# Self-attention of a transformer block: one copy of keys and queries, sums by accumulating DMAs, blocks of eight and eight score matmuls

## Chip, core and metric

The kernel runs on one core of a Trainium2 chip. The metric is the device time of one execution in microseconds (us).

## The reference, cut to what matters

```python
def block_forward(x, codebook_embeds, codebook_mask, ...):
    xn = layer_norm(x, ln0_w, ln0_b)
    q, k, v = jnp.split(xn @ qkv_w.T, 3, axis=-1)
    q, k, v = (_heads(q), _heads(k), _heads(v))          # 16 heads of 32 features
    attn = jnp.einsum('bhnd,bhmd->bhnm', q, k) * SCALE
    attn = jax.nn.softmax(attn, axis=-1)
    x = x + _merge(jnp.einsum('bhnm,bhmd->bhnd', attn, v)) @ sa_proj_w.T
    ...
```

`x` is 2 batches of 2048 tokens with 512 features, in float32. A cross-attention with 154 keys and an MLP follow. The change touches the softmax attention of the tokens among themselves alone, `self_phase`.

## The kernel before

The kernel is a row of phases with a barrier between them: `token_phase` (norm and products for queries, keys and values), `self_phase`, `context_phase`, `token_phase`, the cross `attention_phase`, `token_phase`, `mlp_phase`. Every float32 operand of a product is carried as a high and a low part.

`self_phase` works through 32 stages. A stage is 512 queries (`TOK`) of one batch for four heads (a group of 128 features, each head on its own 32 features), against all 2048 keys; four stages share the keys of a group (`stages_per_group`). A stage i has these parts, and the engines run them as an order written out by hand, each engine in its own function with waits on semaphores:

- **First pass** (`first_pass`, L1466, matmul L1472): scores with the queries in rows, 64 matmuls of 96x128 weights against 512 keys. VectorE (`maxima`, L1585) reduces each to a maximum per query (L1591). The results lie in `first`, a ring of three PSUM banks (`ring`, `in_ring`), and `slot_free` says which reduce has to be over before a slot is written again. `turn_max` (L1475) transposes the maxima in a slot of the same ring, `split_max` (L1598) splits them in two parts, and two DMAs (`load_max`, L1351, on SyncE's queue) lay them as rows 96 and 97 beside the queries.
- **Second pass** (`second_pass`, L1480, matmul L1489): the scores again with the keys in rows, less the maxima by the two extra rows, 64 matmuls of 98x128 weights against 512 queries. ScalarE (L1562) takes the exponential of each into `expo`, a ring of eight key tiles of four heads. `second` too is a ring of three PSUM banks.
- **Values** (`weigh`, L1492, matmul L1500): one key tile of exponentials against the values, four matmuls of 32 columns side by side for the four heads, accumulated in `weighted`. Such a float32 matmul shows as two records in the profile, so a group is x8 there.
- **Sums** (GpSimd's `add_pairs`, L1443; `add_up`, L1504, matmul L1510): GpSimd adds the exponentials of two key tiles (eight "pair" adds of 128x2048 elements, L1453) and merges some pairs once more (two "merge" adds, L1457). TensorE adds each of the six results over the keys, as four matmuls with ones side by side, into `total`.
- **Finish**: VectorE inverts `total` in four pieces (`invert`, L1606, L1610) and multiplies (`divide`, L1612, L1616), ScalarE having copied the weighted values (`take_weighted`, L1565); SyncE stores (`store_out`).

TensorE's order (`period`, L1523) sets the rest: a stage is 16 blocks (`blocks`); a block alternates four first-pass matmuls with four second-pass matmuls (`per_block`), and `batch` (L1514) closes it with the value group of one key tile and, after the blocks that `sums_after` names, a sum:

```python
                def period(i, with_last, with_next, with_after):
                    for j in range(blocks):
                        for at in range(per_block):
                            of, n = first_of[j][at]
                            if with_next if of == 1 else with_after:
                                first_pass(i + of, n)
...
                            second_pass(i, j * per_block + at)
                        batch(i, j, with_last, True)
```

The first pass runs ahead: in the blocks of stage i stand the first-pass matmuls of stage i + 1 from its seventeenth on, and in the last four blocks the first sixteen of stage i + 2; the turn of the maxima lies in block 12. VectorE's four inverse pieces stand in blocks 3 to 6 and the division in block 7, each after the block's second reduce. SyncE's queue loads keys and queries twice, once for each pass (`k_move`, `q_hold` for the first, `k_hold`, `q_move` for the second), each as three copies of 32 rows (high, high, low or high, low, high), and issues each load when the waits in its order have passed.

Of the kernel before, what the change touches and what calls it, by code (L numbers as in the profile page):

```python
# [6 lines left out]
P = 128  # L7
ALU = mybir.AluOpType
ACT = mybir.ActivationFunctionType
F32 = mybir.dt.float32  # L10
# [6 lines left out]
TOK = 512  # L17
# [1169 lines left out]
def self_phase(nc, name, q_t, k_t, v, out, batches):  # L1187
# [16 lines left out]
    blocks = n_k  # L1204
    per_block = heads
# [5 lines left out]
    pair_slots = 4  # L1211
# [6 lines left out]
    sum_ready = [pool_ops.index(("merge", p) if ("merge", p) in pool_ops else ("pair", p)) + 1 for p in summed]  # L1218
    n_sums = len(summed)
    sums_after = {1: [(-1, 4)], 2: [(-1, 5)], 8: [(0, 0)], 9: [(0, 1)], 11: [(0, 2)], 15: [(0, 3)]}  # L1220
    slot_sum = {0: [0, 3], 1: [1], 2: [4], 3: [2, 5]}
# [31 lines left out]
    with ExitStack() as stack:  # L1253
        m = Memory(nc, stack, name)
        k_move = m.sbuf("k_move", [P, heads, keys], F32R)
        k_hold = m.sbuf("k_hold", [P, heads, keys], F32R)
        q_hold = m.sbuf("q_hold", [P, heads, TOK], F32R)
        q_move = m.sbuf("q_move", [P, 2, heads, TOK], F32R)
# [19 lines left out]
        k_move_loaded = [m.sem(f"k_move_loaded{a}") for a in range(heads)]  # L1278
        k_hold_loaded = [m.sem(f"k_hold_loaded{j}") for j in range(4)]
        v_loaded = [m.sem(f"v_loaded{j}") for j in range(4)]  # L1280
        q_hold_loaded = [m.sem(f"q_hold_loaded{a}") for a in range(heads)]
        q_move_loaded = m.sem("q_move_loaded")
# [8 lines left out]
        pool_done = m.sem("pool_done")  # L1291
# [16 lines left out]
        with nc.Block() as block:  # L1308

            @block.sync  # L1310
            def _(sp):
# [8 lines left out]
                def load_k_move(g, a):  # L1320
                    b, group = group_of(g)
                    stacked(k_move[:, a:a + 1], k_t, (0, 0, 1), bass.ds(group * P + a * HEAD_DIM, HEAD_DIM),
                            bass.ds(b * keys, keys), k_move_loaded[a])

                def load_k_hold(g, j):
                    b, group = group_of(g)
                    k0, n = j * k_set * P, k_set * P
                    stacked(k_hold[:, :, k0:k0 + n], k_t, (0, 0, 1), bass.ds(group * P, P), bass.ds(b * keys + k0, n),
                            k_hold_loaded[j])
# [720 lines left out]
```

## Time and profile before

| | before |
|---|---|
| median of 3 runs (lowest to highest) | 3913.47 us (3911.08 to 3914.4) |
| the profiled execution, its own time | 3913.35 us |
| its span, first to last instruction | 3911.6 us |
| TensorE busy in the span | 3591.7 us (92%) |
| VectorE, ScalarE, GpSimd busy | 2221.3, 1601.9, 1731.8 us |
| reduces L1591 | 2048, 1265.2 us busy |
| exponentials L1562 | 2048, 1074.2 us busy |
| score matmuls L1472 and L1489 | 2048 and 2048 |
| value matmuls L1500, records | 4096, 545.5 us busy |
| sum matmuls L1510, records | 1536, 201.6 us busy |
| GpSimd's adds L1453 and L1457 | 256 and 64, 1170.2 and 293.4 us busy |

A busy time counts an engine once however many of its instructions overlap; matmuls are pipelined, so the time from one start to the next says more than their duration. An "idle before" with an arrow names what ended the wait. The self-attention spans about 316 to 2168 us.

### The profile page before, as it was taken

The numbers are of one execution on the slowest core, as the hardware profiler recorded it, in microseconds if no ns is written. First come the engines' busy times: TensorE is split into PE (matmuls) and PEld (weight loads), VectorE is DVE, ScalarE is ACT, GpSimd is POOL, SyncE is SP. The second block draws the span as 40 slices with busy tenths as digits, with TensorE's granted clock in tenths as the row PEclk, the third lists the DMA queues.
The fourth block names the chain that finished last, engine by engine and source line by source line (L and its number), as shares of the span: only waits on it lengthen the run. The fifth ranks groups of instructions, "written<-read, shape, count | busy, mean of one in ns | idle before, by whom it ended". The sixth has DMA issues, their size and how long they took to land. (4 is left out here: it accounts for less than half of the span.)

```text
span 3911.6 us, 57974 instructions
## 1 busy us (share of the span) xinstructions
PE 3591.7 (92%) x17160; PEld 2143.7 (55%) x17160; DVE 2221.3 (57%) x3649; ACT 1601.9 (41%) x2855; POOL 1731.8 (44%) x415
## 2 busy tenths in 40 slices
PE   7998999999999999999999499599996859999999
PEld 6884444444444444444443377334332748888887
DVE  4446777777777777778773344345553743222222
ACT  3221666666666666666566233033333331111111
POOL 0001878887888788878888121132233300000000
PEclk9996999999999999999999699555555979999999
DMA  4546132232313132232410434865743662111110
GB/s 168 181 156 155 36 88 50 69 74 59 80 44 87 41 81 63 65 74 53 92 32 9 157 133 168 181 131 123 149 91 107 240 223 88 43 44 43 43 43 22
DMA packets 197952, 370.25 MB, mean 95 GB/s; under 512 B 28706, under 2 KB 53048, under 8 KB 188652
## 3 DMA queue, kind: packets, MB, share of 16 engines
q1 hardware_dynamic: 197868, 369.15, 34.0%
q8 instruction: 50, 0.82, 0.1%
q14 instruction: 34, 0.28, 0.0%
HBM read 248.68 MB, written 119.34 MB: 94 GB/s over the span
## 5 line engine op out<-in xcount | busy, mean ns | idle before, releaser
L1591 DVE TENSOR_REDUCE self_part_max<-self_first 128x1 f32<-128x512 f32 x2048 | 1265.2, 680 | 378.4 <-PE self_first L1472 375.5
L1562 ACT ACTIVATE self_expo<-self_second 128x512 f32<-128x512 f32 x2048 | 1074.2, 602 | 754.6 <-PE self_second L1489 754.6
L1453 POOL TENSOR_TENSOR self_pair_sum<-self_expo 128x2048 f32<-128x2048 f32 x256 | 1170.2, 4576 | 365.6 <-ACT self_expo L1562 365.6
L1472 PE MATMUL self_first<-self_k_move,self_q_hold 96*128 96x512 f32 x2048 | 895.2, 444 | 31.3 <-DVE self_part_max L1591 18.8
L1489 PE MATMUL self_second<-self_q_move,self_k_hold 98*128 (+1 forms) x2048 | 812.4, 400 | 4.3 <-ACT self_expo L1562 4.2
L1472 PEld LDWEIGHTS self_first<-self_k_move,self_q_hold 96*128 96x128 f32 x2048 | 393.9, 193 | 587.7 <-DVE self_part_max L1591 308.9
L1500 PE MATMUL self_weighted<-self_expo,self_v_sb 128*32 128x512 f32 x4096 | 545.5, 604 | 10.0 <-issue 10.0
L1489 PEld LDWEIGHTS self_second<-self_q_move,self_k_hold 98*128 98x128 f32 x2048 | 388.7, 191 | 84.7 <-ACT self_expo L1562 24.8
L1943 DVE CAST mlp_h_high<-mlp_h 128x512 fp32r<-128x512 f32 x128 | 54.7, 427 | 504.6 <-PE mlp_out_sum L61 504.6
L1918 ACT ACTIVATE mlp_h<-mlp_hidden_sum,mlp_b_col 128x512 f32<-128x512 f32 x128 | 88.0, 688 | 601.0 <-PE mlp_hidden_sum L61 601.0
L937 POOL TENSOR_TENSOR cross_pair_sum<-cross_expo 77x2048 f32<-77x2048 f32 x32 | 144.7, 4521 | 358.8 <-ACT cross_expo L1072 358.8
L1457 POOL TENSOR_TENSOR self_pair_sum<-self_pair_sum 128x2048 f32<-128x2048 f32 x64 | 293.4, 4585 | 5.0
L1072 ACT ACTIVATE cross_expo<-cross_second 77x512 f32<-77x512 f32 x256 | 144.4, 590 | 301.7 <-PE cross_second L992 301.4
L59 PE MATMUL mlp_hidden_sum<-mlp_xt_high,mlp_w_high 128*128 128x512 f32 x512 | 201.2, 393 | 24.1 <-DMA mlp_xt_low<-xn_t 24.1
L968 PEld LDWEIGHTS cross_first<-cross_k_move,cross_q_hold 98*128 98x128 f32 x512 | 137.8, 318 | 148.7 <-issue 83.8
L968 PE MATMUL cross_first<-cross_k_move,cross_q_hold 98*128 98x154 f32 x512 | 152.2, 422 | 62.2 <-DMA cross_k_move<-mask_rows 39.7
L1510 PE MATMUL self_total<-self_pair_sum,self_ones 128*32 128x512 f32 x1536 | 201.6, 595 | 5.1 <-POOL self_pair_sum L1453 5.1
L1124 DVE TENSOR_REDUCE cross_row_max<-cross_first 128x2 f32<-128x308 f32 x256 | 115.6, 472 | 159.3 <-PE cross_first L968 157.7
L59 PE MATMUL mlp_out_sum<-mlp_w_high,mlp_h_high 128*128 128x512 f32 x512 | 202.6, 396 | 0.0
L60 PE MATMUL mlp_out_sum<-mlp_w_low,mlp_h_high 128*128 128x512 f32 x512 | 202.5, 396 | 0.0
L61 PE MATMUL mlp_hidden_sum<-mlp_xt_high,mlp_w_low 128*128 128x512 f32 x512 | 202.5, 395 | 0.0
L61 PE MATMUL mlp_out_sum<-mlp_w_high,mlp_h_low 128*128 128x512 f32 x512 | 202.4, 395 | 0.0
(163 smaller groups left out, 4187.7 us busy)
## 6 DMA issues: line engine op xcount, KB each, us to landing
self_q_hold<-q_t SPq DMA_DIRECT2D x384, 64.0 KB, 2.1
self_k_move<-k_t SPq DMA_DIRECT2D x96, 256.0 KB
self_q_move<-q_t SPq DMA_DIRECT2D x96, 256.0 KB, 4.5
self_k_hold<-k_t SPq DMA_DIRECT2D x96, 256.0 KB, 4.7
cross_q_hold<-cq_t SPq DMA_DIRECT2D x24, 1024.0 KB, 12.0
cross_q_move<-cq_t SPq DMA_DIRECT2D x24, 1024.0 KB, 14.5
qkv_x<-in_x SPq DMA_DIRECT2D x8, 1024.0 KB, 5.7
v<-qkv_v_sb SPq DMA_DIRECT2D x32, 256.0 KB, 2.0
```

The source lines that it names most:

```text
L59: nc.tensor.matmul(out, left_high, right_high, start=first, stop=False)
L60: nc.tensor.matmul(out, left_high, right_low, start=False, stop=False)
L61: return nc.tensor.matmul(out, left_low, right_high, start=False, stop=last)
L968: mm = nc.tensor.matmul(first[:, n % ring, half * keys:(half + 1) * keys], q_hold[0:score_rows, a, (s + half) * P:(s + half + 1) * P], k_m ...
L1453: nc.gpsimd.tensor_tensor(pair_sum[:, p % pair_slots], expo[:, t % p_slots], expo[:, (t + 1) % p_slots], ALU.add).then_inc(pool_done, 1)
L1457: nc.gpsimd.tensor_tensor(pair_sum[:, p % pair_slots], pair_sum[:, p % pair_slots], pair_sum[:, (p + 1) % pair_slots], ALU.add).then_inc(p ...
L1472: nc.tensor.matmul(first[:, in_ring[n]], q_hold[0:base, a, s * P:(s + 1) * P], k_move[0:base, a, k0:k0 + TOK], start=True, stop=True).then ...
L1489: nc.tensor.matmul(second[:, n % ring], k_hold[0:exp_rows, a, t * P:(t + 1) * P], q_move[0:exp_rows, i % 2, a], start=True, stop=True).the ...
L1500: mm = nc.tensor.matmul(weighted[cols], v_sb[:, t, cols], expo[:, t % p_slots, a], start=t == 0, stop=t == n_k - 1)
L1510: mm = nc.tensor.matmul(total[cols], ones[:], pair_sum[:, summed[n] % pair_slots, a], start=n == 0, stop=n == n_sums - 1)
L1562: nc.scalar.activation(expo[:, t % p_slots, a], second[:, n % ring], ACT.Exp, scale=scale).then_inc(exp_done, 1)
L1591: nc.vector.tensor_reduce(part_max[:, a * SUB + s, k:k + 1], first[:, in_ring[n]], AX_X, ALU.max).then_inc(first_read, 1)
```

## The change

- **One copy.** `k` (two buffers, one for each group of keys in flight) and `q` (four slots, one a stage) replace the four tensors; both passes read the same bytes, the first their 96 rows and the second 98. Keys are loaded a whole group ahead and queries three stages ahead, at the start of a stage. The constant rows of the keys are set once for each buffer.
- **Blocks.** A stage is eight blocks of eight and eight score matmuls, still alternating, and each block's batch holds two value groups. The inverse pieces stand in blocks 3 to 6 of eight, the division in block 7, the turn of the maxima in block 6.
- **Sums.** There are two sums a stage instead of six: one over `half_sum[0]` after block 7 (`early_sum`), one over `half_sum[1]` after block 2 of the next stage (`late_sum`). GpSimd writes pairs 0 and 1 straight into the two halves; pairs 2 and 4 are added to the first, and 3, 5 and 6 to the second, each by a DMA from GpSimd's queue that accumulates from SBUF into SBUF (128 partitions of 8 KB, 1 MB); pair 7 is added by GpSimd itself at the end.
- **Maxima.** ScalarE's queue issues the two DMAs of the maxima, after block 6, in place of SyncE's.
- **Loops.** The order repeats over rounds of eight stages, since the slots of `q` and the buffers of `k` are fixed numbers in the code; the body of TensorE's, ScalarE's and SyncE's loop is eight stages long.

```diff
-    blocks = n_k
-    per_block = heads
+    blocks = n_k // 2
+    per_block = 2 * heads
-    pool_ops = [("pair", 0), ("pair", 1), ("pair", 2), ("merge", 1), ("pair", 3), ("pair", 4), ("pair", 5), ("merge", 4),
-                ("pair", 6), ("pair", 7)]
-    summed = [0, 1, 3, 4, 6, 7]
-    sums_after = {1: [(-1, 4)], 2: [(-1, 5)], 8: [(0, 0)], 9: [(0, 1)], 11: [(0, 2)], 15: [(0, 3)]}
+    q_slots = 4
+    round_stages = 2 * stages_per_group
+    n_sums = 2
+    n_adds = n_pairs + 1
+    late_sum, early_sum, invert_from, max_sent = 2, 7, 3, 6
...
+        k = m.sbuf("k", [P, 2, heads, keys], F32R)
+        q = m.sbuf("q", [P, q_slots, heads, TOK], F32R)
-        pair_sum = m.sbuf("pair_sum", [P, pair_slots, heads, TOK])
+        pair_sum = m.sbuf("pair_sum", [P, 2, heads, TOK])
+        half_sum = m.sbuf("half_sum", [P, 2, heads, TOK])
...
+                def add_half(i, p, u, part):
+                    ge(pool, pair_done, n_adds * i + p + 1, alone=True)
+                    pool.dma_start(half_sum[:, u].rearrange("p a t -> p (a t)"),
+                                   pair_sum[:, part].rearrange("p a t -> p (a t)"), accum_op=ALU.add).then_inc(
+                        half_added[u], 16)
...
+                    ge(pool, total_done, n_sums * i - 1)
+                    add_pair(i, 0, half_sum[:, 0])
+                    ge(pool, total_done, n_sums * i)
+                    add_pair(i, 1, half_sum[:, 1])
+                    ge(pool, half_added[1], 48 * i)
+                    add_pair(i, 2, pair_sum[:, 0])
+                    add_half(i, 2, 0, 0)
+                    ge(pool, pair_done, n_adds * i)
+                    add_pair(i, 3, pair_sum[:, 1])
+                    add_half(i, 3, 1, 1)
+                    ge(pool, half_added[0], 32 * i + 16)
+                    add_pair(i, 4, pair_sum[:, 0])
+                    add_half(i, 4, 0, 0)
+                    ge(pool, half_added[1], 48 * i + 16)
+                    add_pair(i, 5, pair_sum[:, 1])
+                    add_half(i, 5, 1, 1)
+                    ge(pool, half_added[0], 32 * i + 32)
+                    add_pair(i, 6, pair_sum[:, 0])
+                    ge(pool, half_added[1], 48 * i + 32, alone=True)
+                    add_half(i, 6, 1, 0)
+                    add_pair(i, 7, pair_sum[:, 1])
+                    ge(pool, half_added[1], 48 * i + 48)
+                    ge(pool, pair_done, n_adds * i + n_pairs)
+                    nc.gpsimd.tensor_tensor(half_sum[:, 1], half_sum[:, 1], pair_sum[:, 1], ALU.add).then_inc(
+                        pair_done, 1)
...
                 def add_up(i, n):
                     if n == 0:
                         ge(pe, mean_done, i)
-                    ge(pe, pool_done, len(pool_ops) * i + sum_ready[n])
+                        ge(pe, half_added[0], 32 * (i + 1))
+                    else:
+                        ge(pe, pair_done, n_adds * (i + 1))
...
+                def batch(r, c, j, with_last, with_this):
+                    for t in range(tiles_of * (j - 1), tiles_of * j):
+                        if t >= 0 and with_this:
+                            weigh(r, c, t)
+                        if t < 0 and with_last:
+                            weigh(r, c - 1, t + n_k)
+                    if j == late_sum and with_last:
+                        add_up(round_stages * r + c - 1, 1)
+                    if j == early_sum and with_this:
+                        add_up(round_stages * r + c, 0)
...
-                            if with_last and 3 <= j < 3 + pieces and at == 1:
-                                invert(i - 1, j - 3)
-                            if with_last and j == 3 + pieces and at == 1:
+                            if with_last and invert_from <= j < invert_from + pieces and at == 1:
+                                invert(i - 1, j - invert_from)
+                            if with_last and j == invert_from + pieces and at == 1:
                                 divide(i - 1)
```

TensorE's order before, from one value group of stage 0 to the next (`self_first` and `self_second` are the two passes' scores):

```order
L1500 MATMUL self_weighted<-self_expo,self_v_sb 32x512 x4
L1472 MATMUL self_first<-self_k_move,self_q_hold 128x512
L1489 MATMUL self_second<-self_q_move,self_k_hold 128x512
L1472 MATMUL self_first<-self_k_move,self_q_hold 128x512
L1489 MATMUL self_second<-self_q_move,self_k_hold 128x512
L1472 MATMUL self_first<-self_k_move,self_q_hold 128x512
L1489 MATMUL self_second<-self_q_move,self_k_hold 128x512
L1472 MATMUL self_first<-self_k_move,self_q_hold 128x512
L1489 MATMUL self_second<-self_q_move,self_k_hold 128x512
L1500 MATMUL self_weighted<-self_expo,self_v_sb 32x512 x4
L1472 MATMUL self_first<-self_k_move,self_q_hold 128x512
```

The same place after the change, its first twelve rows:

```order
L1484 MATMUL self_weighted<-self_expo,self_v_sb 32x512 x8
L1455 MATMUL self_first<-self_k,self_q 128x512
L1471 MATMUL self_second<-self_q,self_k 128x512
L1455 MATMUL self_first<-self_k,self_q 128x512
L1471 MATMUL self_second<-self_q,self_k 128x512
L1455 MATMUL self_first<-self_k,self_q 128x512
L1471 MATMUL self_second<-self_q,self_k 128x512
L1455 MATMUL self_first<-self_k,self_q 128x512
L1471 MATMUL self_second<-self_q,self_k 128x512
L1455 MATMUL self_first<-self_k,self_q 128x512
L1471 MATMUL self_second<-self_q,self_k 128x512
L1455 MATMUL self_first<-self_k,self_q 128x512
```

The value matmuls stand eight together instead of four, and sixteen score matmuls lie between one batch and the next instead of eight.

GpSimd's order in stage 0, before (the pairs and merges into `self_pair_sum`):

```order
L1453 TENSOR_TENSOR self_pair_sum<-self_expo 128x2048 x3
L1457 TENSOR_TENSOR self_pair_sum<-self_pair_sum 128x2048
L1453 TENSOR_TENSOR self_pair_sum<-self_expo 128x2048 x3
L1457 TENSOR_TENSOR self_pair_sum<-self_pair_sum 128x2048
L1453 TENSOR_TENSOR self_pair_sum<-self_expo 128x2048 x2
```

And after:

```order
L1402 TENSOR_TENSOR self_half_sum<-self_expo 128x2048 x2
L1402 TENSOR_TENSOR self_pair_sum<-self_expo 128x2048
L1407 DMA self_half_sum<-self_pair_sum 128x2048
L1402 TENSOR_TENSOR self_pair_sum<-self_expo 128x2048
L1407 DMA self_half_sum<-self_pair_sum 128x2048
L1402 TENSOR_TENSOR self_pair_sum<-self_expo 128x2048
L1407 DMA self_half_sum<-self_pair_sum 128x2048
L1402 TENSOR_TENSOR self_pair_sum<-self_expo 128x2048
L1407 DMA self_half_sum<-self_pair_sum 128x2048
L1402 TENSOR_TENSOR self_pair_sum<-self_expo 128x2048
L1407 DMA self_half_sum<-self_pair_sum 128x2048
L1402 TENSOR_TENSOR self_pair_sum<-self_expo 128x2048
```

Two merges have gone, one add at the end has come, and after each of the pairs 2 to 6 a DMA is issued.

## Rows read from the trace of the kernel before

**Rows 1.** Busy time in one stage: us, then each engine, TensorE clock, DMA share, GB/s

```profile
1201.00:1257.00 56.00, 55.12 (x306) 26.54 (x306) 43.93 (x73) 33.98 (x66) 45.74 (x11) 1.00 0.38 85
```

**Rows 2.** Order of time, TensorE matmuls: start us, us, engine, line, what, [idle before]

```profile
1201.37 1.07 PE L1500 MATMUL self_weighted<-self_expo,self_v_sb 128*32 128x512 f32 x8
...
1205.42 0.50 PE L1472 MATMUL self_first<-self_k_move,self_q_hold 96*128 96x512 f32 x1
1205.76 0.40 PE L1489 MATMUL self_second<-self_q_move,self_k_hold 98*128 x1
...
1207.16 0.39 PE L1489 MATMUL self_second<-self_q_move,self_k_hold 98*128 x1
1207.48 1.06 PE L1500 MATMUL self_weighted<-self_expo,self_v_sb 128*32 128x512 f32 x8
1208.47 0.50 PE L1472 MATMUL self_first<-self_k_move,self_q_hold 96*128 96x512 f32 x1
...
1210.53 1.07 PE L1500 MATMUL self_weighted<-self_expo,self_v_sb 128*32 128x512 f32 x8
...
1212.38 0.50 PE L1472 MATMUL self_first<-self_k_move,self_q_hold 96*128 96x512 f32 x1
...
1254.29 0.50 PE L1472 MATMUL self_first<-self_k_move,self_q_hold 96*128 96x512 f32 x1
...
1256.50 0.40 PE L1489 MATMUL self_second<-self_q_move,self_k_hold 98*128 x1
...
1257.32 1.07 PE L1500 MATMUL self_weighted<-self_expo,self_v_sb 128*32 128x512 f32 x8
```

**Rows 3.** Order of time, VectorE, same stage

```profile
1205.96 2.48 DVE L1591 TENSOR_REDUCE self_part_max<-self_first 128x1 f32<-128x512 f32 x4 [0.57 <-PE self_first L1472]
...
1228.63 0.96 DVE L1610 RECIPROCAL self_total<-self_total 128x128 f32<-128x128 f32 x1
1229.49 2.41 DVE L1591 TENSOR_REDUCE self_part_max<-self_first 128x1 f32<-128x512 f32 x4
...
1238.22 0.68 DVE L1616 TENSOR_TENSOR self_mean<-self_total,self_unscaled 128x512 f32<-128x512 f32 x1
1238.82 3.67 DVE L1591 TENSOR_REDUCE self_part_max<-self_first 128x1 f32<-128x512 f32 x6
...
1254.83 1.29 DVE L1591 TENSOR_REDUCE self_part_max<-self_first 128x1 f32<-128x512 f32 x2 [1.19 <-PE self_first L1472]
...
1256.70 0.69 DVE L1591 TENSOR_REDUCE self_part_max<-self_first 128x1 f32<-128x512 f32 x1
```

**Rows 4.** Order of time, weight loads of TensorE, same stage

```profile
1256.17 0.19 PEld L1472 LDWEIGHTS self_first<-self_k_move,self_q_hold 96*128 96x128 f32 x1 [0.88 <-DVE self_part_max L1591]
```

**Rows 5.** Order of time, ScalarE, one block

```profile
1206.19 2.06 ACT L1562 ACTIVATE self_expo<-self_second 128x512 f32<-128x512 f32 x4 [0.99 <-PE self_second L1489]
```

**Rows 6.** Groups of instructions, GpSimd's adds: busy us, mean ns, idle before

```profile
L1453 POOL TENSOR_TENSOR self_pair_sum<-self_expo 128x2048 f32<-128x2048 f32 x256 | 1170.2, 4576 | 365.6 <-ACT self_expo L1562 365.6
```

**Rows 7.** DMA issues: queue, count, size, median us to landing

```profile
cross_q_move<-cq_t SPq DMA_DIRECT2D x24, 1024.0 KB, 14.5
...
out<-mlp_x SPq DMA_DIRECT2D x8, 1024.0 KB, 4.2
```

**Rows 8.** One line's instructions: issues of the maxima, min/median/max ns, and their landing

```profile
L1354 SPq DMA_DIRECT2D self_q_move<-self_max_low x32: 576/583/592, 366.6 to 2095.6; - x32
...
DMA to landing us min/median/max: 1.8/1.8/3.2
```

**Rows 9.** Busy time of a stretch of loads, same columns as rows 1

```profile
2170.00:2180.00 10.00, 0.00 (x0) 0.00 (x0) 3.10 (x2) 4.11 (x3) 0.00 (x0) 0.50 0.76 270
```

**Rows 10.** Order of time, TensorE, start of the last stage

```profile
2104.97 0.96 PE L1489 MATMUL self_second<-self_q_move,self_k_hold 98*128 98x512 f32 x3
...
2107.58 0.97 PE L1489 MATMUL self_second<-self_q_move,self_k_hold 98*128 98x512 f32 x3
```

**Rows 11.** Order of time, GpSimd, its last adds

```profile
2150.49 9.01 POOL L1453 TENSOR_TENSOR self_pair_sum<-self_expo 128x2048 f32<-128x2048 f32 x2
```

More of the change, by code:

```diff
@@ L1290, in self_phase @@
         exp_done = m.sem("exp_done")
-        pool_done = m.sem("pool_done")
+        pair_done = m.sem("pair_done")
+        half_added = [m.sem(f"half_added{u}") for u in range(2)]
         weighted_done = m.sem("weighted_done")
@@ L1363, in period @@
                     number = i if isinstance(i, int) else None
-                    has_next = number is None or number < stages - 1
-                    has_after = number is None or number < stages - 2
-                    new_next = (qt + 1) % stages_per_group == 0 and has_next
-                    new_after = (qt + 2) % stages_per_group == 0 and has_after
-                    after = (i + 2) // stages_per_group if number is not None else g + 1
-                    def heads_free(a):
-                        if has_after:
-                            ge(sp, first_done, n_items * (i + 1) + per_head * (a + 1), alone=True)
-                            load_q_hold(i + 2, a)
-                            if new_after:
-                                load_k_move(after, a)
@@ L1377, in k_free @@
-                    def k_free(j):
-                        if new_next:
-                            ge(sp, second_done, n_seconds * i + heads * k_set * (j + 1), alone=True)
-                            load_k_hold(g + 1, j)
+                    g, qt = 2 * r + c // stages_per_group, c % stages_per_group
+                    last_group = number is not None and number >= stages - stages_per_group
                     def v_free(j):
-                        if new_next:
+                        if qt == stages_per_group - 1 and not last_group:
@@ L1392, in period @@
+                    if qt == 0 and not last_group:
+                        for a in range(heads):
+                            load_k(g + 1, (c // stages_per_group + 1) % 2, a)
                     if qt == 0 and number != 0:
@@ L1563, in exponential, with load_max @@
                         exp_done, 1)
+                def load_max(r, c):
+                    ge(act, first_read, reads_until_turned(round_stages * r + c), alone=True)
+                    for row, src in ((base, max_high), (base + 1, max_low)):
+                        act.dma_start(q[row:row + 1, c % q_slots].rearrange("o a (s t) -> o (a s) t", t=P).bitcast(F32),
+                                      src[:].bitcast(F32)).then_inc(max_loaded, 16)
                 def take_weighted(i):
@@ L1574, in period @@
                             take_weighted(i - 1)
-                period(0, False)
-                with act.Fori(1, stages) as i:
-                    period(i, True)
+                        if n == (max_sent + 1) * per_block - 1 and with_next:
+                            load_max(r, c + 1)
+                load_max(0, 0)
+                period(0, 0, False, True)
+                with act.Fori(0, rounds - 1) as r:
+                    for c in range(1, round_stages + 1):
+                        period(r, c, True, True)
+                for c in range(1, round_stages):
+                    period(rounds - 1, c, True, c < round_stages - 1)
                 take_weighted(stages - 1)
```

220 lines of the change are left out of this document (88 added, 132 removed).

## The prediction

> **What bounds the kernel now.** I read the busy time of a stretch first, then the order of time of TensorE beside VectorE, its weight loads and ScalarE, then GpSimd's groups and the DMA. The self-attention runs 32 stages. In one of them TensorE is busy for 55.1 of 56 us at clock 1.00, VectorE for 43.9, GpSimd for 45.7 and ScalarE for 34.0 [rows 1]. From one batch to the same one of the next stage a stage takes 1257.32 - 1201.37 = 55.95 us [rows 2]. So TensorE binds, and what counts is its order of time.
>
> In a block the first score matmul starts at 0, the next at 0.34, and then one follows every 0.234 us (1205.42, 1205.76 and six more to 1207.16) [rows 2]. The value batch starts 0.32 after the last one, and the next block 1.00 after that, with a sum in between 1.85 (1207.16, 1207.48, 1208.47; 1210.53, 1212.38) [rows 2]. A block of four and four is thus 3.05 us, of which 0.32 lie between score and value matmuls; a further group costs about 0.86 (a batch with a sum less one without). By TensorE alone the change would take away four sums and eight changes of kind a stage: 4 x 0.86 + 8 x 0.32 = 6.0 us.
>
> But the score matmuls write a ring of three, which VectorE empties. It starts 0.54 after the block's first matmul (1205.42 to 1205.96) [rows 2, 3], takes 0.68 for one and starts the next after (3.67 - 0.68) / 5 = 0.60 [rows 3]. TensorE issues one for it every 0.47. The weight load of a first score matmul waits for the reduce three back: it starts 0.05 after that ends (1254.83 + 1.29 = 1256.12 against 1256.17), and the score matmul behind it 0.33 after the load [rows 2 to 4]. Four in a row end before this is felt; eight don't.
>
> **The change, part by part.** *A block of eight and eight.* Reduce k ends at 1.22 + 0.60 k. The eighth first matmul needs reduce 4, at 3.62; its load starts at 3.67 and the last second matmul at 4.00, where alone it would be at 0.34 + 7 x 0.47 = 3.62. Then 0.32, 0.86 and 1.00: 6.18 us, against 6.10 for two old blocks. The 0.32 saved is given back. ScalarE takes an exponential every (2.06 - 0.60) / 3 = 0.49 [rows 5] and stays inside this.
>
> *The inverse and the division.* A reciprocal pushes the reduces behind it by 0.86, the division by 0.60 (1228.63 to 1229.49, 1238.22 to 1238.82) [rows 3]. They keep their number, in blocks 3 to 6 and 7, after the second reduce. Before, VectorE idled 0.57 in a block and had a 3.20 us rhythm there, so each cost some 0.1. Now each stands before reduce 4 and goes whole into TensorE's wait: 7.03 for such a block (with 0.58 between reduces, (2.41 - 0.68) / 3), and 6.76 with the division.
>
> *The turn of the row maxima* (block 6). The third first matmul reuses the slot of the second and waits for its reduce; the split ends, and the next reduce starts, 2.41 after the block's start (1254.29, 1256.70) [rows 2, 3]. A reciprocal behind it puts reduce 2 at 3.27 and reduce 4 at 4.43 to 5.11, so the last second matmul is at 5.49 and the block lasts 7.67.
>
> *Sum of a stage:* blocks 0 and 1 take 6.18 + 6.23 (ScalarE's copy of the weighted values falls in the second and costs 0.05), block 2 with a sum 7.04, blocks 3 to 5 21.09, block 6 7.67, block 7 with division and sum 7.62: **55.83**, against 55.95. The six microseconds are gone in VectorE's ring: 29 full stages, -3 us.
>
> *GpSimd and the accumulating DMAs.* Nine adds of 4.58 [rows 6] for ten, and five DMAs a stage of 1 MB each. One round of dependences runs through merge, pair 0, pair 1 (which waits for the late sum), pair 2, its DMA, pair 4, its DMA, pair 6 (or 5), the last DMA, and the next merge: six adds, about four issues c and three landings D: 27.5 + 4c + 3D. If that is less than 55.8 it hides under TensorE, since the early sum stands at the end of block 7 and the late one at the end of block 2. The trace has no issue from GpSimd and no accumulating transfer. For c the nearest row is SyncE's 0.58 [rows 8]; between nothing and one add of 4.6 I take 0.6. For D the ends are 4.2 for 1 MB stored and 14.5 for 1 MB that queued with others [rows 7]. An accumulation reads source and target: 2 MB at 270 / 0.76 = 355 GB/s [rows 9] are 5.9 us, and a transfer of 8 KB lands in 1.8 [rows 8]: D = 7.7 (an estimate). The round is then 27.5 + 2.4 + 23.1 = 53.0 us, just hidden; at the lower end 42.5, at the upper 73.4.
> The Trainium skill (DMA: Bandwidth & Descriptors, Anatomy of one DMA) gives 2.0 us and the bytes over 436 GB/s, 4.4 us for 1 MB, and does not count the second stream; with it the round would be 43 us and the last stage 10 us shorter, so about 3910 us in all.
>
> *Loads.* The second copies of keys and queries fall away. They lay beside other work (TensorE waited for loads only before stage 0), and the first heads still load in the same order: 0. If the cover went, one key load would be felt in every fourth stage. The two DMAs of the maxima move from SyncE to ScalarE, after the exponentials of block 6: 1.2 us of issue [rows 8], in a gap of about 2 us until the next one is due, and a landing in 1.8 us, with a whole block to spare: 0.
>
> *The ends.* Stage 0 has no reciprocals: 8 x 6.18 + 0.86 + 0.6 for the turn = 50.9, against 16 x 3.05 + 4 x 0.86 + 1.0 = 53.2: -2.3. Stage 30 loses its first matmuls from block 6 on: about -1. The last stage has none, and ends on GpSimd. Before, GpSimd's last add ended at 2150.49 + 9.01 = 2159.50, 54.5 us after the stage began at 2104.97 [rows 10, 11]. Now its blocks last 5.4 (twice 2.61 [rows 10], with exponentials every 0.49 for 0.2 more), so the late sum frees pair 1 at 17.2. Pair 2 ends at 26.4 and lands at 34.7; pair 4 ends at 39.3 and lands at 47.6; pair 5 lands at 52.8 and lets pair 6's DMA go, which lands at 61.1; the merge ends at 65.7. What follows it is as before. +11.2.
>
> **Sum:** -3 - 2.3 - 1 + 11.2 = +5 us on 3913.35 us of the profiled execution (median of the runs 3913.47): about 3918; I add 2 us for key loads that cross a landing in every fourth stage and give **3920 us**. A measurement tells about 0.2% (7.8 us) from no change.
>
> **Rivals.**
> *VectorE does not hold TensorE.* Then 6 us a stage are kept, 3913 - 31 x 6 + 5 = about 3732. For it: VectorE idles 12 us of 56. Against it: that idle time falls in the value batches, and the load at 1256.17 shows that the ring does hold [rows 4]. 6%. If the waits are half as long, 3825; 3% for that.
> *The round of DMAs sets the stage* (the slow side). It decides from D = (55.8 - 27.5 - 2.4) / 3 = 8.6 us, at the early sum, for which TensorE then waits with its scores queued behind. With D = 10 a stage is 59.9: 3913 + 31 x 4.1 + 15 = about 4055; every further microsecond of D is 93 us. For it: D is only 0.9 below the point, loads of 1 MB reach 14.5 us. Against it: those queued behind others, and the plain one takes 4.2. 28%.
> *The traffic crosses.* 5 MB a stage more, where a stage moved 4.8 MB (85 GB/s [rows 1]). If maxima or keys land late by 3 us in one stage of two, +45: 3965. 7%.
> The Trainium skill (Trainium Kernel Development and Optimization, Key Constraints) says that DMAs of all issuing engines share the same 16 engines and interleave; that is this last mechanism.
> *It does nothing at all* is what the sum nearly says, and is inside the forecast.
>
> **How the numbers follow.** Forecast 56%, its own range 3902 to 3940 (0.4 us a stage either way is 12 us, D from 4.2 to 8.6 is 13 us in the last stage). Within it 6% lie below 3905.7, 27% within 0.2%, 23% above 3921.3. With the rivals: faster 0.15 (6 + 6 + 3), same 0.27, slower 0.58 (23 + 28 + 7). The range leaves out the fast rivals and the slow half of the DMA rival, D above 10: 3895 to 4060. The upper bound of D would give 3913 + 31 x 17.6 = about 4460 and lies in the part left out.
>
> **What would show it.** In the profile after: score blocks in which the load of a first matmul waits for a reduce, some 0.4 us a block and 1.2 with a reciprocal; 6.2 and 7.0 us between batches; two sums a stage; VectorE and TensorE busy for about the same time a stage as before; GpSimd 41 us and the issues. If blocks last 5.8 us, the ring step is wrong. If TensorE waits for the sum on a DMA or on GpSimd, D or c is. The landing of the accumulating DMA is the number to look at first.

## The result and the profile after

| | before | after |
|---|---|---|
| median (lowest to highest) | 3912.95 us (3911.08 to 3914.4) | 3976.55 us (3969.69 to 3984.54) |
| the profiled execution, its own time and span | 3913.35 and 3911.6 us | 3974.24 and 3972.5 us |

The change makes the kernel slower by 1.6%: ratio 1.0164, 95% interval 1.0143 to 1.0184. Forecast 3920 us, range 3895 to 4060: the sign and the range held, the forecast's own range (3902 to 3940) did not.

The 32 turns of the row maxima (`self_identity`, once a stage) mark the stages on TensorE. Stages are counted from 0, and a distance between two turns is given to the stage in which it ends. The first stands at 364.02 before and 364.56 after, the last at 2093.99 and 2137.54 (their rows in both traces). Between them lie 31 distances. Before, all but the first and the last are 55.91 to 56.02 us. After, the first two and the last are shorter than that, most are 55.54 to 55.66, and eight are longer:

| stages | distance, us | over 55.6 |
|---|---|---|
| 4, 8, 12, 16, 20 and 24, in which the next group's keys are loaded | 57.65, 62.63, 65.27, 63.23, 63.1, 65.25 | 43.5 in sum |
| 9 and 17, behind the jump back of the loop | 62.73, 63.5 | 15.0 in sum |
| the first two | 48.17, 54.37 | -8.7 |

From the last turn to the end of the last division (VectorE's timeline) it is 71.7 us before (the division starts at 2164.98 and takes 0.69) and 86.8 after (2223.64 and 0.69). So the +60.9 us of the profiled execution are: the start +0.5, the stages without the excess of the table -15.6 (1772.98 - 43.5 - 15.0 = 1714.4 between the turns, against 1729.97), key loads +43.5, jumps +15.0, the last stage +15.1, and some 2 us elsewhere.

*A quiet stage.* TensorE's timeline after, columns as in [rows 2]: from the value batch of one block to that of the next. The batches shown close blocks 1 to 6.

```profile
1240.56 1.92 PE L1484 MATMUL self_weighted<-self_expo,self_v_sb 128*32 128x512 f32 x16
...
1246.76 1.92 PE L1484 MATMUL self_weighted<-self_expo,self_v_sb 128*32 128x512 f32 x16
1248.50 1.04 PE L1496 MATMUL self_total<-self_half_sum,self_ones 128*32 128x512 f32 x8
...
1254.61 1.92 PE L1484 MATMUL self_weighted<-self_expo,self_v_sb 128*32 128x512 f32 x16
...
1261.61 1.92 PE L1484 MATMUL self_weighted<-self_expo,self_v_sb 128*32 128x512 f32 x16
...
1268.61 1.92 PE L1484 MATMUL self_weighted<-self_expo,self_v_sb 128*32 128x512 f32 x16
...
1276.10 1.92 PE L1484 MATMUL self_weighted<-self_expo,self_v_sb 128*32 128x512 f32 x16
```

A plain block lasts 6.20 us (block 2), one with a reciprocal 7.00 (blocks 4 and 5), the one with the turn and a reciprocal 7.49 (block 6). Block 3 has the late sum in front of it besides. And inside one of them, matmuls and then weight loads:

```profile
1256.47 0.50 PE L1455 MATMUL self_first<-self_k,self_q 96*128 96x512 f32 x1
...
1258.44 0.40 PE L1455 MATMUL self_first<-self_k,self_q 96*128 96x512 f32 x1
1258.68 0.40 PE L1471 MATMUL self_second<-self_q,self_k 98*128 98x512 f32 x1
1259.75 0.50 PE L1455 MATMUL self_first<-self_k,self_q 96*128 96x512 f32 x1 [0.67 <-DVE self_part_max L1595]
...
1261.61 1.47 PE L1484 MATMUL self_weighted<-self_expo,self_v_sb 128*32 128x512 f32 x9
```

The weight loads there:

```profile
1258.34 0.19 PEld L1455 LDWEIGHTS self_first<-self_k,self_q 96*128 96x128 f32 x1 [0.18 <-DVE self_part_max L1595]
...
1259.75 0.19 PEld L1455 LDWEIGHTS self_first<-self_k,self_q 96*128 96x128 f32 x1 [1.11 <-DVE self_part_max L1595]
```

The fifth second-pass matmul starts at 1258.68, the next first-pass one only at 1259.75: its load waited 1.11 us for a reduce. It is the wait of [rows 4], now in each block. The windows answer to [rows 1]; the columns are the same:

```profile
1187.00:1243.00 56.00, 52.73 (x276) 25.49 (x277) 43.55 (x73) 34.93 (x65) 46.74 (x15) 1.00 0.56 114
1303.00:1310.00 7.00, 1.27 (x12) 0.13 (x4) 0.42 (x1) 0.05 (x1) 4.43 (x1) 0.96 1.03 233
1312.00:1316.00 4.00, 4.00 (x14) 3.14 (x11) 3.02 (x5) 1.99 (x4) 4.00 (x2) 0.50 0.38 65
879.00:885.00 6.00, 0.77 (x8) 0.00 (x0) 0.00 (x0) 0.00 (x0) 1.63 (x3) 0.81 0.98 187
```

In a whole stage TensorE is busy for 52.73 us of 56 instead of 55.12; the freed time has become waiting. The DMA share rose from 0.38 to 0.56. The other stretches are read below.

*The round of GpSimd and DMA.* GpSimd's timeline, first a quiet stage, then one with key loads:

```profile
1187.25 4.60 POOL L1435 TENSOR_TENSOR self_half_sum<-self_half_sum,self_pair_sum 128x2048 f32<-128x2048 f32 x1 [2.89 <-DMA self_half_sum<-self_pair_sum]
...
1200.87 4.58 POOL L1402 TENSOR_TENSOR self_pair_sum<-self_expo 128x2048 f32<-128x2048 f32 x1
1206.03 0.88 POOL L1407 DMA_DIRECT2D self_half_sum<-self_pair_sum  x1 [0.58 <-POOL self_pair_sum L1402]
1206.64 4.88 POOL L1402 TENSOR_TENSOR self_pair_sum<-self_expo 128x2048 f32<-128x2048 f32 x1
...
1224.82 0.87 POOL L1407 DMA_DIRECT2D self_half_sum<-self_pair_sum  x1 [0.58 <-POOL self_pair_sum L1402]
...
1234.42 0.88 POOL L1407 DMA_DIRECT2D self_half_sum<-self_pair_sum  x1 [3.77 <-DMA self_half_sum<-self_pair_sum]
1235.03 4.89 POOL L1402 TENSOR_TENSOR self_pair_sum<-self_expo 128x2048 f32<-128x2048 f32 x1
1241.76 4.59 POOL L1435 TENSOR_TENSOR self_half_sum<-self_half_sum,self_pair_sum 128x2048 f32<-128x2048 f32 x1 [1.84 <-DMA self_half_sum<-self_pair_sum]
...
1281.88 4.56 POOL L1402 TENSOR_TENSOR self_pair_sum<-self_expo 128x2048 f32<-128x2048 f32 x1 [0.58 <-DMA self_half_sum<-self_pair_sum]
1289.87 0.88 POOL L1407 DMA_DIRECT2D self_half_sum<-self_pair_sum  x1 [3.43 <-DMA self_half_sum<-self_pair_sum]
1290.47 4.89 POOL L1402 TENSOR_TENSOR self_pair_sum<-self_expo 128x2048 f32<-128x2048 f32 x1
1305.57 4.49 POOL L1435 TENSOR_TENSOR self_half_sum<-self_half_sum,self_pair_sum 128x2048 f32<-128x2048 f32 x1 [10.21 <-DMA self_half_sum<-self_pair_sum]
```

SyncE's queue in the second of these stages:

```profile
1286.84 7.67 SPq L1312 DMA_DIRECT2D self_k<-k_t  x12
```

TensorE at the end of it:

```profile
1302.35 1.92 PE L1484 MATMUL self_weighted<-self_expo,self_v_sb 128*32 128x512 f32 x16
1310.12 1.93 PE L1496 MATMUL self_total<-self_half_sum,self_ones 128*32 128x512 f32 x8 [5.85 <-POOL self_half_sum L1435]
...
1312.58 0.63 PE L1471 MATMUL self_second<-self_q,self_k 98*128 98x512 f32 x1
1313.00 0.63 PE L1455 MATMUL self_first<-self_k,self_q 96*128 96x512 f32 x1
```

Twelve key loads are issued from 1286.84 on, behind the stage's three query loads and among three loads of values. The accumulating DMA of 1289.87 lands after 15.6 us instead of some 7, and the merge that waits for it starts at 1305.57. It ends at 1310.06, and TensorE, which had its late sum next in order, stood for 5.85 us. The DMA engines were busy all the while (1303 to 1310 in the windows, share 1.03). It then goes on with a matmul every 0.43 us instead of 0.234 [rows 2]: from 1312 to 1316 the granted clock is 0.50, 1.2 GHz instead of 2.4, and from 1316.35 on a matmul starts every 0.234 us again. In the quiet stage the same merge ended at 1246.35, 2.15 us ahead of the sum at 1248.50. That is the slack of this merge. The issues' own line:

```profile
L1407 POOL DMA_DIRECT2D self_half_sum<-self_pair_sum x160: 874/877/1073, 397.2 to 2206.6; - x160
...
DMA to landing us min/median/max: 6.9/7.4/17.0
```

The waits between 600 and 1900 us (us in total, times, longest):

```profile
PEld self_total L1496 <- POOL self_half_sum L1435: 37.0, 7, 7.7
...
PE self_first L1455 <- issue: 10.9, 2, 5.5
```

*The jump.* TensorE's timeline where its loop of eight stages goes back to its start:

```profile
878.73 1.04 PE L1496 MATMUL self_total<-self_half_sum,self_ones 128*32 128x512 f32 x8
885.29 0.79 PE L1455 MATMUL self_first<-self_k,self_q 96*128 96x512 f32 x1 [5.52 <-issue]
885.87 0.63 PE L1471 MATMUL self_second<-self_q,self_k 98*128 98x512 f32 x1
886.30 0.63 PE L1455 MATMUL self_first<-self_k,self_q 96*128 96x512 f32 x1
```

The profile shows nothing that TensorE waits for, but 5.52 us pass, and the next matmuls run at half the clock too. The DMA share is 0.98 there (879 to 885 in the windows), and the queue that brings instructions moved 50 packets before and 125 after (part 3 of the page).

### The profile page after: what moved, and what is told of

Same layout as the page of the kernel before. It is cut to its first block and busy times, and to the rows that moved or that the text cites. A ratio compares the mean times of both kernels' runs of the same rounds, so it can differ in the third digit from the quotient of the medians.

```text
span 3972.5 us, 53244 instructions
## 1 busy us (share of the span) xinstructions
PE 3536.0 (89%) x16136; PEld 2118.0 (53%) x16136; DVE 2211.9 (56%) x3649; ACT 1632.7 (41%) x2855; POOL 1730.9 (44%) x542
## 5 line engine op out<-in xcount | busy, mean ns | idle before, releaser
L1455 PE MATMUL self_first<-self_k,self_q 96*128 96x512 f32 x2048 | 941.2, 467 | 119.6 <-DVE self_part_max L1595 96.1
L1402 POOL TENSOR_TENSOR self_pair_sum<-self_expo 128x2048 f32<-128x2048 f32 x192 | 902.8, 4702 | 48.3 <-DMA self_half_sum<-self_pair_sum 31.9
L1471 PE MATMUL self_second<-self_q,self_k 98*128 98x512 f32 x2048 | 832.4, 408 | 3.5 <-ACT self_expo L1553 3.4
L1455 PEld LDWEIGHTS self_first<-self_k,self_q 96*128 96x128 f32 x2048 | 399.4, 195 | 658.8 <-DVE self_part_max L1595 521.0
L1471 PEld LDWEIGHTS self_second<-self_q,self_k 98*128 98x128 f32 x2048 | 395.4, 193 | 79.8 <-ACT self_expo L1553 31.6
L1402 POOL TENSOR_TENSOR self_half_sum<-self_expo 128x2048 f32<-128x2048 f32 x64 | 291.8, 4577 | 65.4 <-ACT self_expo L1553 50.6
L1484 PEld LDWEIGHTS self_weighted<-self_expo,self_v_sb 128*32 128x32 f32 x4096 | 107.6, 110 | 247.7 <-issue 170.9
L1407 POOL DMA_DIRECT2D self_half_sum<-self_pair_sum x160 | 140.6, 879 | 176.0 <-DMA self_half_sum<-self_pair_sum 99.6
L1435 POOL TENSOR_TENSOR self_half_sum<-self_half_sum,self_pair_sum 128x2048 f32<-128x2048 f32 x32 | 146.3, 4572 | 140.2 <-DMA self_half_sum<-self_pair_sum 140.2
L60 PE MATMUL mlp_hidden_sum<-mlp_xt_low,mlp_w_high 128*128 128x512 f32 x512 | 202.7, 396 | 0.0
```

What stands on the lines that cost most here:

```text
L60: nc.tensor.matmul(out, left_high, right_low, start=False, stop=False)
L1402: nc.gpsimd.tensor_tensor(to, expo[:, t % p_slots], expo[:, (t + 1) % p_slots], ALU.add).then_inc(pair_done, 1)
L1435: nc.gpsimd.tensor_tensor(half_sum[:, 1], half_sum[:, 1], pair_sum[:, 1], ALU.add).then_inc(pair_done, 1)
L1455: nc.tensor.matmul(first[:, in_ring[n]], q[0:base, c % q_slots, a, s * P:(s + 1) * P], k[0:base, c // stages_per_group % 2, a, k0:k0 + TOK ...
L1471: nc.tensor.matmul(second[:, n % ring], k[0:exp_rows, c // stages_per_group % 2, a, t * P:(t + 1) * P], q[0:exp_rows, c % q_slots, a], sta ...
L1484: mm = nc.tensor.matmul(weighted[cols], v_sb[:, t, cols], expo[:, t % p_slots, a], start=t == 0, stop=t == n_k - 1)
```

## The experiments

Each is an edit of the changed kernel, and distances are between turns as above. Two things ask for a stage's time: TensorE with its ring, and GpSimd's round of adds and DMAs. The experiments take from the one or the other.

### The key loads: spread over the stages

```diff
-                    if qt == 0 and not last_group:
-                        for a in range(heads):
-                            load_k(g + 1, (c // stages_per_group + 1) % 2, a)
+                    if not last_group:
+                        load_k(g + 1, (c // stages_per_group + 1) % 2, qt)
```

> The twelve key loads of a group, issued together at the start of every fourth stage, are issued three a stage instead. If they are what stretches the landing of an accumulating DMA (17 us at most against 7.4) and so the merge that the late sum waits for, the seven long stages that have them (57.7 to 65.3 us) fall to 55.6 but for the two at the loop's end: 3976 - 43 = about 3933. Rival: 1 MB accumulations are too slow beside any load; then the same bytes spread out make more stages a little longer and the time stays within 10 us of 3976.

Measured: 4019.57 us, ratio to the kernel before 1.0271 (1.0254 to 1.0288), 43 us above the change. My forecast fell, and the rival's bound of 10 us too, though its mechanism is what came: every distance from stage 3 to stage 27 is longer now, 56.6 to 68.1 us. (The long stages with key loads in the changed kernel are six, not seven.) The waits of the sum for the merge, same view and columns:

```profile
PEld self_total L1495 <- POOL self_half_sum L1434: 68.0, 20, 5.7
```

20 waits in place of 7. A landing that meets a load is late, and the round has next to no slack for even a small delay: the burst is paid once in four stages, the spread load in nearly all.

### Without the accumulating DMAs

Left out are the five DMAs of a stage and their waits, so the sums lack pairs 2 to 6.

```diff
-                    pool.dma_start(half_sum[:, u]..., pair_sum[:, part]..., accum_op=ALU.add).then_inc(
-                        half_added[u], 16)
...
-                        ge(pe, half_added[0], 32 * (i + 1))
+                        ge(pe, pair_done, n_adds * i + 5)
```

> Leaves out the five accumulating DMAs of a stage and the waits on them, so the sums lack pairs 2 to 6; all adds and sum matmuls stay. If VectorE's ring alone sets a stage without key loads, stages stay at 55.6 us, the long ones fall to that, the two at the loop's end stay at 63, and the last stage ends 15 us earlier: about 3976 - 43 - 15 = 3918. Rival: the round of DMAs already holds the stage at 55.6; then all stages get shorter, by up to 4 us each, and the time is near 3800 to 3850.

Measured: 3907.85 us, 0.9983 (0.9973 to 0.9992). From the third to the last but one the distances are 55.55 to 55.66, key loads or not, and 57.0 behind the jumps. So the ring alone holds the stage at 55.6, and the DMAs cost 55.5 us between the turns (1772.98 - 1717.5) and 9.9 in the last stage (86.8 - 76.9). I had expected the stages behind the jumps to stay at 63; they fell too. TensorE at its first jump:

```profile
869.84 1.04 PE L1487 MATMUL self_total<-self_half_sum,self_ones 128*32 128x512 f32 x8
872.22 0.50 PE L1446 MATMUL self_first<-self_k,self_q 96*128 96x512 f32 x1 [1.33 <-issue]
...
872.79 0.40 PE L1446 MATMUL self_first<-self_k,self_q 96*128 96x512 f32 x1
```

1.33 us for the same jump, where 5.52 pass beside the DMAs. That the instructions themselves come late because the DMA engines are taken (share 0.98) fits this and the queue's packets, but it was only argued, and the run with three sums below speaks against it as the whole cause.

### The reciprocals at the end of their blocks

```diff
-                            if with_last and invert_from <= j < invert_from + pieces and at == 1:
+                            if with_last and invert_from <= j < invert_from + pieces and at == per_block - 1:
```

> Each reciprocal stands after the last reduce of its block instead of after the second, in the time in which VectorE idles. If a reciprocal in front of the fifth reduce goes whole into TensorE's wait, blocks 3 to 6 fall from 7.0 to 6.2 us and a stage could be 52.2; GpSimd's own round, counted from the trace (six adds 27.5, three landings with their issues 27.5, in all 55 to 55.5), would then bind, and a stage falls only to about 55: 3976 - 10 to 20. If GpSimd's round has slack, 3976 - 31 x 3.4 = 3870. If the reciprocals did not matter, 3976 within 5.

Measured: 3976.39 us, 1.0142 (1.0118 to 1.0166). Eight stages fall to 52.5 to 52.6, as the ring step says. But the others grow to between 54 and 68, and the mean stays (1773.9 us between the first turn and the last, against 1773.0). The time is that of "the reciprocals did not matter", the reason is not; the 10 to 20 us that I expected did not come. What TensorE gains in one stage it gives back at the sum of another, so the round, with its late landings, takes about as long as the stages did:

```profile
PEld self_total L1496 <- POOL self_half_sum L1435: 106.9, 17, 14.1
```

### TensorE's loop written out

```diff
-                with pe.Fori(0, rounds - 1) as r:
+                for r in range(rounds - 1):
```

> TensorE's loop over rounds of eight stages is written out, the other engines' loops stay. If the jump back costs TensorE the two waits of 5.5 us in which nothing releases it (plus the slower clock behind them), stages 9 and 17 fall from 62.7 and 63.5 to 55.6: 3976 - 15 = 3961. Rival: these waits come from the loads of the stage; then nothing changes.

Measured: 3968.24 us, 1.0133 (1.0116 to 1.015). The two distances stay at 62.84 and 64.72; the 8 us gained lie in the six stages with key loads (33.5 us over 55.6 in sum instead of 43.5). ScalarE's timeline there:

```profile
888.45 1.57 ACT L1553 ACTIVATE self_expo<-self_second 128x512 f32<-128x512 f32 x3 [6.29 <-issue]
```

ScalarE's own loop of eight stages has taken the place. With it written out too, beside the edit above:

```diff
-                with act.Fori(0, rounds - 1) as r:
+                for r in range(rounds - 1):
```

> The changed kernel with the loops of TensorE and of ScalarE written out, nothing else. With TensorE's alone the two long stages at the loop's end stayed at 62.8 and 64.7 us because ScalarE's jump took its place. Now both fall to 55.6: 3976 - 15 = about 3961, and the stages with key loads stay long. If it is the load of q or the store in that stage, nothing changes.

Measured: 3951.31 us, 1.009 (1.0073 to 1.0106). The two distances are 55.65 and 55.61: the jumps' 15 us are gone. Those of the key loads stay longer (61.68, 63.53, 57.37, 64.17, 57.04, 63.36), though by 33.5 us in sum as in the run before. These 10 us are the rest of the gain over the change; why two of the six shrank by 6 and 8 us when TensorE's loop was written out stays open.

### Blocks of four and four, without the DMAs

As the second experiment (the sums lack pairs 2 to 6), with the blocks of before.

```diff
-    blocks = n_k // 2
-    per_block = 2 * heads
+    blocks = n_k
+    per_block = heads
-    late_sum, early_sum, invert_from, max_sent = 2, 7, 3, 6
+    late_sum, early_sum, invert_from, max_sent = 5, 15, 6, 13
```

> Sixteen blocks of four and four again, with one value group each, the two sums and all else of the change; the accumulating DMAs are left out, as in the run without them, so the sums lack pairs 2 to 6. If blocks of eight cost what two blocks of four cost and only push the reciprocals into TensorE's wait, a stage is 16 x 3.05 + 2 x 0.86 + 0.4 + 1.0 + 0.4 = 52.3 us against 55.6: 3908 - 31 x 3.3 = about 3806. Rival: the longer value batch saved 0.32 us eight times a stage; then it is 55.6 + 2.6 - 4.0 = 54.2, 3865.

Measured: 3816.66 us, 0.9754 (0.9738 to 0.977); distances 52.42 to 52.6 but for the first, the last and those behind the jumps. Against the same without the fours, 3.1 us a stage. So "eight and eight", with the reciprocals behind the second reduce, is a loss by itself, and most of what the fewer sums gain (55.95 - 52.5) goes into it.

### DMAs that copy instead of accumulating

```diff
-                                   pair_sum[:, part].rearrange("p a t -> p (a t)"), accum_op=ALU.add).then_inc(
+                                   pair_sum[:, part].rearrange("p a t -> p (a t)")).then_inc(
```

> The five DMAs of a stage copy instead of accumulating (same bytes, queue and waits), so the sums lack what they would add. If the accumulation reads a second stream, the copy lands in 1.8 + 1 MB at 355 GB/s = 4.8 us instead of 7.4, the round has 8 us of slack, and the time falls to that of the run without the DMAs, 3908 to 3920. Rival: the landing is set by GpSimd's way of issuing or by the crossing loads; then the copy lands in 7 us too and the time stays at 3976.

Measured: 3919.6 us, 1.0013 (1.0003 to 1.0023). The same bytes in the same places land in 4.6 us, and an issue takes 0.57:

```profile
L1407 POOL DMA_DIRECT2D self_half_sum<-self_pair_sum x160: 567/567/740, 396.2 to 2154.7; - x160
...
DMA to landing us min/median/max: 4.3/4.6/10.3
```

A landing is then over before the next add is, and GpSimd's own order sets its round: nine adds and five times 1.18 us from one add to the next are 47 us. It now waits for TensorE's sum instead (the waits between 600 and 1900 us):

```profile
POOL self_half_sum L1402 <- PE self_total L1496: 151.2, 23, 10.0
```

The stages of the key loads are 55.6 like the rest: the loads hurt through the round. The jumps still cost 5.5 and 5.2 us, so they don't need a round without slack.

### Three sums in place of the merge

Pair 7 is summed by TensorE straight from `pair_sum[1]`, and the merge falls away. That takes one add and one landing out of GpSimd's round and gives TensorE one more sum.

```diff
-    n_sums = 2
-    n_adds = n_pairs + 1
+    n_sums = 3
+    n_adds = n_pairs
...
-                    nc.gpsimd.tensor_tensor(half_sum[:, 1], half_sum[:, 1], pair_sum[:, 1], ALU.add).then_inc(
-                        pair_done, 1)
...
+                        add_up(round_stages * r + c - 1, 2)
```

> Pair 7 is not merged into the second half by GpSimd but summed by TensorE itself, so there are three sums a stage and eight adds on GpSimd. GpSimd's round of dependences loses an add of 4.6, the wait in front of it and the wait of the sum on it, and has some 6 us of slack. If the want of slack is what makes key loads visible, the stages with key loads fall to within 4 us of the others, and a stage becomes 55.6 + 0.9: 3976 + 31 x 0.9 - 35 - 8 in the last stage = about 3960. Rival: it is the number of bytes beside each other that counts; then the long stages stay and the time goes up, to 4000.

Measured: 3941.48 us, 1.0069 (1.0053 to 1.0086); all distances 56.42 to 56.5 but the first two, the last and those behind the jumps (59.4). With a landing of 7.2 us in the median and 16.3 at most, as slow as before, the excess of the key loads is gone. It was the missing slack. TensorE's first jump in this run, and the windows there:

```profile
878.17 0.49 PE L1451 MATMUL self_first<-self_k,self_q 96*128 96x512 f32 x1 [1.72 <-issue]
876.00:878.00 2.00, 0.45 (x7) 0.00 (x0) 0.00 (x0) 0.00 (x0) 1.75 (x2) 1.00 1.10 237
```

The accumulating DMAs are all there and the DMA share is 1.10, but the jump takes 1.72 us and not 5.52. So full DMA engines alone don't make a jump long; what does stays open.

### Everything together

The edits above taken together, with the DMAs accumulating and nothing left out: three sums, reciprocals late, keys spread, both loops written out.

> Three sums, reciprocals behind the last reduce of their block, key loads three a stage, and the loops of TensorE and ScalarE written out. If ring, round of DMAs and the jump are all that held the changed kernel, a stage is 52.5 + 0.9 = 53.4 us throughout, with at most 1 us more where a key load crosses: 365 + 31 x 53.5 and an end some 75 us behind the last turn, so the span is near 3972 - 113 - 12 = 3848: about 3850, below both kernels. Rival: with 5 MB of accumulations a stage some landing is always late; then stages scatter from 54 to 60 and the time is 3900 to 3960.

Measured: 3847.04 us (3843.89 to 3850.16), 0.9828 (0.9811 to 0.9844): **faster than both kernels**, by 1.7% against the one before. Its window of a whole stage:

```profile
1200.00:1254.00 54.00, 52.97 (x289) 25.42 (x281) 44.40 (x73) 33.99 (x65) 41.59 (x14) 1.00 0.70 147
```

TensorE is busy for 52.97 of 54 us, the distances from the third on are 53.41 to 53.6, but for 53.85, 54.37 and the last. The same with the keys in one burst again:

> As the version with three sums, reciprocals moved, spread key loads and loops written out (3847 us), but with the key loads in one burst of twelve every fourth stage, as in the change. The round of DMAs has about 6 us of slack at 53.4 us a stage; a burst stretches one landing by up to 10 us. So stages with a burst should be up to 4 us longer, 7 x 2 to 4: 3860 to 3875. If slack alone mattered and it is enough, 3847 within 3.

Measured: 3865.75 us, 0.9872 (0.9855 to 0.9888); the six stages are 54.9, 57.69, 54.94, 57.35, 57.05, 58.67. The edit that cost 43 us in the first experiment now gains 19: with slack in the round a small delay is swallowed and a large one isn't. And the first of these two with the edit of the fours above, without the late reciprocals:

> Sixteen blocks of four and four with one value group each, three sums, key loads three a stage, both loops written out; the reciprocals stand after the second reduce of their block as in the change. Without DMAs this order gave stages of 52.5 and a span of 3813.5 us; one more sum a stage adds 0.87, 27 us, and the DMAs 5 to 8 in the last stage: about 3848, the same as eight and eight with the reciprocals moved (3847). If the longer value batch has any merit of its own, this one is slower by 0.3 us a stage, 3857; if the eight and eight only cost, it is faster, 3840.

Measured: 3850.29 us, 0.9833 (0.9816 to 0.9849). So eights with the reciprocals where VectorE idles and fours with them where they were are the same within 0.1%.

## Why the prediction was right or wrong

- **A block of eight and eight: right.** Forecast 6.18, 7.03, 6.76 and 7.67 us; measured 6.20, 7.00, 6.79 (1220.53 to 1227.32) and 7.49. The stage comes out at 55.6 where the sum gave 55.83. That the gain of the fewer sums goes into VectorE's ring is shown by the fours (-3.1 us a stage) and by the late reciprocals (-3.05, in the stages that don't wait for the sum).
- **D, the landing of an accumulating DMA: right.** 7.7 forecast, 7.4 measured as the median. By the figures of the Trainium skill (DMA: Bandwidth & Descriptors, Anatomy of one DMA) an estimate for 1 MB is 4.4 us; the copying DMA agrees with 4.6, the accumulating one doesn't.
- **c, the price of an issue: too small.** I took 0.6. GpSimd waits 0.58 us from its add to the issue, the next add starts 0.61 after that, 1.19 in all (1205.45, 1206.03, 1206.64), and shows 4.88 instead of 4.58. The round can be followed in the quiet stage from the merge at 1187.25 to that at 1241.76. Its path goes through pairs 3 and 5 and not 2 and 4: six adds 27.7, landings of 7.4, 8.9 and 7.2, and 3.4 around the issues, 54.5 us instead of 53.0. "Just hidden" by 2.8 us was hidden by about one.
- **"Key loads: 0", with 2 us added for those that cross a landing: the step that failed.** The term measured 43.5 us, 41.5 of the 56.6 by which the time was missed. I looked for a wait for the keys; between the first turn and the last none comes. The loads lengthen the landing of the accumulating DMAs (15.6 us), and these were the one thing next to without slack. The rival "the traffic crosses" had the crossing right (3 us in one stage of two, 3965 us) and its victims wrong, maxima or keys, and its 7% was too little. The Trainium skill (Trainium Kernel Development and Optimization, Key Constraints) says that DMAs issued from all queues run on the same 16 DMA engines and interleave; the trace agrees, with a DMA share of 1.03 while SyncE's loads and GpSimd's DMA were under way. My sum had no term for it.
- **That the range up to 4060 held is luck.** Its slow half was made for landings above 8.6 us in every stage; here it took up late landings in six stages and two jumps. The sign was forecast from a last stage that came out longer still, but three quarters of the loss lie elsewhere.
- **The loops: not priced.** I told of the body of eight stages and gave it nothing: 15 us, shown by writing out the loops of TensorE and ScalarE.
- **The last stage: undersized.** +15.1 instead of 11.2 - 1 = 10.2. From pair 1 to the end of the merge the chain was right (48.0 us, 2170.16 to 2218.15, against 65.7 - 17.2 = 48.5). But pair 1 began 21.1 us after TensorE began the stage (2149.08) and not 17.2: I let it wait for the late sum alone, while the merge of the stage before ended only at 2165.70 and pair 0 came behind it.
- **The other stages: a little better than forecast**, -15.6 instead of -5.3 (-3 and, for stage 0, -2.3). The first two distances give 5.1 of it, the rest 0.36 a stage, where the sum had 0.12.
- **"The round of DMAs sets the stage" did not come true in the quiet stages**, but with the ring made faster by 3 us it does at once (third experiment). Its point of decision was right as a formula and lay nearer than I wrote. I had put the wait at the early sum; it came at the late one, behind the merge.

Not tried: one copy of keys and queries by itself, the part of the value loads that stand beside the key loads, and the part of the lower clock in the key-load stages by itself. The cause of the long jumps is open too.

## What to carry to other kernels

Count a round of dependences through DMAs with the time that an issue blocks its engine, and compare it with the stage not at the median landing but at the landing beside the heaviest load; a slack of 2 us is none when 1 MB can take 17. With no slack spread loads cost more than a burst, with slack less, so the same edit must be judged again once the slack has changed. Before runs of matmuls are lengthened to save changes of kind, look whether the engine that empties their ring keeps pace within the run, and put its occasional work where it would idle.

## What the hardware showed that I had not expected

- An accumulating DMA of 1 MB within SBUF lands in 7.4 us (6.9 to 17.0), a copying one in 4.6 (4.3 to 10.3); its issue shows 0.88 us on GpSimd against 0.57.
- At the jump back of a loop of eight stages TensorE stands for 1.3 to 1.4 us without the DMAs of GpSimd (1.9 to 2.1 with blocks of four), for 5.4 to 5.5 with them and for 4.0 to 4.3 when they copy. But it stands for only 1.7 with them and three sums, and with late reciprocals once for 1.6 and once for 4.7. ScalarE stands for 5.8 to 6.3 at its own when TensorE's loop is written out.
- After 5.85 us without work TensorE went on at half its clock for 6 us (the sum at 1310.12 takes 1.93 instead of 1.04; full speed from 1316.35), in a stage that was 7.6 us over.
- The second of the two small DMAs of the maxima, 0.58 us to issue on SyncE [rows 8], takes ScalarE a median of 1.39, and they land after 4.1 instead of 1.8. No time was lost by it that the waits show. Their line's instructions after:

```profile
L1559 ACTq DMA_DIRECT2D self_q<-self_max_low x32: 604/1386/1572, 367.0 to 2141.5; - x32
...
DMA to landing us min/median/max: 1.9/4.1/6.3
```
